# Two layers of pair updates on one core: an affine step cut from four rows to two, and moments of a running output aggregated per sixteen rows

## The reference

```
x = x + L0(_gn(x))      # L0: g * (_ln(einsum('bikc,bkjc->bijc', a, b)) @ Wz + bz),  g = sigmoid(xn @ Wg + bg)
x = x + L1(_gn(x))      # L1: layernorm, p = xn @ pi + b, gate = sigmoid(xn @ gi + b), h = p * gate * mask, triangles, ...
_gn(v) = (v - m) / sqrt(s + 1e-5)   # m, s: mean and variance of a group over all 512 x 512 positions
```

## Time and profile before

| | |
|---|---|
| median of three runs | 4713.67 us (4711.84 to 4716.98) |
| the profiled execution: its own time, its span | 4714.6 us, 4712.9 us |
| mean granted clock of TensorE | 0.975 |
| PE busy | 3987.0 us, 85% |
| DVE busy | 3935.2 us, 83% |
| ACT busy | 3377.8 us, 72% |
| POOL busy | 2670.3 us, 57% |
| HBM traffic over the span | 325 GB/s |

### The profile page before, as it was taken

One profiled execution on the slowest core, in us unless ns is written; L12 is line 12 of the kernel. 1 busy time (PEld: TensorE's weight loads), 2 busy tenths in 40 slices (PEclk: granted clock), 3 DMA queues, 4 the chain that ended last, 5 costly groups with the idle time before them and its releaser, 6 DMA issues. The chain is left out here.

```text
span 4712.9 us, 89415 instructions
## 1 busy us (share of the span) xinstructions
PE 3987.0 (85%) x26438; PEld 2239.9 (48%) x26438; DVE 3935.2 (83%) x5450; ACT 3377.8 (72%) x4840; POOL 2670.3 (57%) x1428
## 2 busy tenths in 40 slices
PE   0008999891999999799999999799999978888888
PEld 0005666441666666455555555355654434444444
DVE  5778888678888888899999999677789978777776
ACT  2337999553777777588888888566667768888887
POOL 0000000591888888588888888733334428888887
PEclk9999999995999999899999999899999989999999
DMA  9997999546999999799999999766678859999999
GB/s 366 410 405 261 364 369 366 176 134 202 392 391 390 390 390 391 268 311 319 321 322 321 320 320 322 271 230 223 231 254 305 305 186 406 407 403 405 403 402 354
DMA packets 700627, 1532.73 MB, mean 325 GB/s; under 512 B 32976, under 2 KB 50832, under 8 KB 698128
## 3 DMA queue, kind: packets, MB, share of 16 engines
q1 hardware_dynamic: 563696, 1263.31, 74.3%
q10 hardware_dynamic: 136864, 268.59, 14.9%
HBM read 1009.59 MB, written 522.19 MB: 325 GB/s over the span
## 5 line engine op out<-in xcount | busy, mean ns | idle before, releaser
L1766 POOL TENSOR_TENSOR s_oT<-s_gated,s7in_x1t 128x1024 f32<-128x1024 f32 x256 | 689.0, 2694 | 220.6 <-DVE s_gated L1685 215.4
L981 POOL TENSOR_TENSOR s_x1T<-s_gz,s_xT 128x512 f32<-128x512 f32 x512 | 652.1, 1274 | 127.9 <-DVE s_gz L947 123.2
L1432 PE MATMUL s_y_ps<-s_ab 128*128 128x512 f16 x3072 | 680.1, 380 | 2.0 <-DVE s_ab L1503 2.0
L1138 POOL TENSOR_TENSOR s_low<-s_xc,s_high 128x1024 f16<-128x1024 f32 x256 | 546.9, 2137 | 222.0 <-ACT s_high L1099 222.0
L878 PE MATMUL s_g_ps<-s_xT,s_Wg 128*128 128x512 f32 x1024 | 523.3, 593 | 0.0
L1685 DVE SCALAR_TENSOR_TENSOR s_gated<-s_p_ps,k_po_bias,s_gate 128x1024 f32<-128x1024 f32 x256 | 328.6, 1284 | 183.7 <-ACT s_gate L1722 164.0
L908 ACT ACTIVATE s_g<-s_g_ps,s_bg 128x512 f32<-128x512 f32 x512 | 351.7, 687 | 174.3 <-PE s_g_ps L878 174.3
L718 POOL MEMSET s_total<- 128x2048 f32 x1 | 1.8, 1809 | 837.9 <-POOLq L41 837.9
L1432 PEld LDWEIGHTS s_y_ps<-s_ab 128*128 128x128 f16 x3072 | 300.9, 98 | 344.8 <-issue 4.4
L947 DVE SCALAR_TENSOR_TENSOR s_gz<-s_z_ps,k_z_bias,s_g 128x512 f32<-128x512 f32 x512 | 384.4, 751 | 88.8 <-ACT s_g L908 86.5
L1104 ACT ACTIVATE s_gate<-s_g_ps,k_gi_bias 128x1024 f32<-128x1024 f32 x256 | 284.1, 1110 | 186.1 <-PE s_g_ps L1272 185.7
(11 more groups left out here) (225 smaller groups left out, 9499.8 us busy)
## 6 DMA issues: line engine op xcount, KB each, us to landing
s2in_xt<-in_x SPq DMA_DIRECT2D x128, 1024.0 KB, 9.6
s_xt<-in_x SPq DMA_DIRECT2D x256, 512.0 KB, 7.3
x_d<-s_x1T ACTq DMA_DIRECT2D x128, 1024.0 KB, 9.6
s5in_xt<-x_d SPq DMA_DIRECT2D x128, 1024.0 KB, 9.1
h_d<-s_h SPq DMA_DIRECT2D x128, 1024.0 KB, 6.8
s7in_x1t<-x_d SPq DMA_DIRECT2D x128, 1024.0 KB, 13.9
out<-s_ot ACTq DMA_DIRECT2D x128, 1024.0 KB, 9.3
s_mask_b<-mask_d SPq DMA_DIRECT2D x128, 512.0 KB, 4.8
```

Of the source, the lines that this page charges most:

```text
L981: pool.tensor_tensor(x1T[:, i // U, i % U, :], gz[:, i % 4, :], xT[:, i % 8, :], ALU.add).then_inc(added, 1)
L1138: pool.tensor_tensor(low[:, n % 4, :, :], xc[:, n % 4, :, :], high[:, n % 4, :, :], ALU.subtract).then_inc(rest_ready, 1)
L1432: last = pe.matmul(y_ps[:, ib, 0:N], ab[:, u % 2, 0, a, kb, ib * P:(ib + 1) * P], ab[:, u % 2, 1, b, kb, :], start=m == 0, stop=m == len(t ...
L1766: pool.tensor_tensor(oT[:, n % 4, :, :], gated[:, n % 4, :, :], x1t[:, n // 2, 2 * (n % 2):2 * (n % 2) + 2, :], ALU.add).then_inc(added, 1)
```

## The change

Stage 4: the tile of statistics holds 16 rows and is used again in every body. At the start of a body DVE waits for the last statistics of the body before, does the mix of row 2, aggregates the 16 rows into a mean and a variance (`gather`, one `bn_aggr` of 96 numbers into `last_mv`), and goes on with statistics of row 0, which wait until `gather` is done. After the statistics of row 1 it copies the two numbers to their place (`place`, a copy of two elements per partition). The body's first statistics find a tile that was set to 1.0 ahead of the loop. At the end of the stage the last 16 rows are gathered, and the 32 means and variances are combined by six short instructions instead of one long and three short ones.

Stage 5: the affine step handles two rows instead of four. It is issued in every step but n = 4 and 12 (with the square root); step 7 and step 15 carry two of them. The total of rows is the same. The affine of a pair waits for the load of its whole group, as before.

```
--- before.py
+++ after.py
@@ -804,8 +804,9 @@
         g = s.sbuf("g", [P, 2, N])
         gz = s.sbuf("gz", [P, 4, N])
         x1T = s.sbuf("x1T", [P, GROUPS, U, N])
-        stats = s.sbuf("stats", [P, N, 6])
-        mv = s.sbuf("mv", [P, 2])
+        stats = s.sbuf("stats", [P, ROWS, 6])
+        last_mv, mv = s.sbuf("last_mv", [P, 2]), s.sbuf("mv", [P, N // ROWS, 2])
+        wide = s.sbuf("wide", [P, 2, N // ROWS])
         pair = s.sbuf("pair", [P, 2])
         Wg = s.sbuf("Wg", [P, P])
         bg = s.sbuf("bg", [P, 1])
@@ -813,8 +814,8 @@
         g_ps = s.psum("g_ps", [P, 2, BANK])
         z_ps = s.psum("z_ps", [P, 2, BANK])
         loaded, z_loaded, stored = s.sems("loaded", GROUPS), s.sems("z_loaded", GROUPS), s.sems("stored", GROUPS)
-        turned, kept, g_prod, z_prod, sig, mixed, added, counted = [
-            s.sem(n) for n in ("turned", "kept", "g_prod", "z_prod", "sig", "mixed", "added", "counted")]
+        turned, kept, g_prod, z_prod, sig, mixed, added, counted, gathered, placed = [
+            s.sem(n) for n in ("turned", "kept", "g_prod", "z_prod", "sig", "mixed", "added", "counted", "gathered", "placed")]
         padded, folded, shifted, moments_ready, chain = s.sem("padded"), s.sem("folded"), s.sem("shifted"), s.sem("moments_ready"), s.sem("chain")
 
         @block_of(nc)
@@ -887,7 +888,7 @@
                 for i in range(ROWS):
                     step(N // ROWS - 1, i, last=True)
 
-                pe.wait_ge(chain, 3)
+                pe.wait_ge(chain, 4)
                 for m in range(2):
                     pe.matmul(moments[:, m:m + 1], K.group_mean[:], pair[:, m:m + 1], start=True, stop=True).then_inc(moments_ready, 1)
 
@@ -935,10 +936,20 @@
 
                 def statistics(r, i):
                     dve.wait_ge(added, r * ROWS + (i + 9))
-                    dve.bn_stats(stats[:, bass.ds(r * ROWS + i, 1), :].rearrange("p a s -> p (a s)"),
-                                 x1T[:, i // U, i % U, :]).then_inc(counted, 1)
-
-                dve.sem_inc(counted, ROWS)
+                    if i == 0:
+                        dve.wait_ge(gathered, r + 1)
+                    if i == U:
+                        dve.wait_ge(placed, r + 1)
+                    dve.bn_stats(stats[:, i, :], x1T[:, i // U, i % U, :]).then_inc(counted, 1)
+
+                def gather():
+                    dve.bn_aggr(last_mv[:], stats[:].rearrange("p n s -> p (n s)")).then_inc(gathered, 1)
+
+                def place(r):
+                    dve.wait_ge(gathered, r + 1)
+                    dve.tensor_copy(mv[:, bass.ds(r, 1), :].rearrange("p a s -> p (a s)"), last_mv[:]).then_inc(placed, 1)
+
+                dve.memset(stats[:], 1.0).then_inc(counted, ROWS)
 
                 def mix(r, i):
                     dve.wait_ge(sig, r * ROWS + (i + 1))
@@ -948,9 +959,15 @@
                                              ALU.add, ALU.mult).then_inc(mixed, 1)
 
                 def step(r, i, last=False):
+                    if i == 0:
+                        dve.wait_ge(counted, r * ROWS + ROWS)
                     if not (last and i + 2 >= ROWS):
                         mix(r, i + 2)
+                    if i == 0:
+                        gather()
                     statistics(r, i)
+                    if i == 1:
+                        place(r)
 
                 mix(0, 0)
                 mix(0, 1)
@@ -960,12 +977,18 @@
                 for i in range(ROWS):
                     step(N // ROWS - 1, i, last=True)
                 dve.wait_ge(counted, N + ROWS)
-                dve.bn_aggr(mv[:], stats[:].rearrange("p n s -> p (n s)")).then_inc(chain, 1)
+                gather()
+                dve.wait_ge(gathered, N // ROWS + 1)
+                dve.tensor_copy(mv[:, 0, :], last_mv[:]).then_inc(placed, 1)
+                dve.wait_ge(placed, N // ROWS + 1)
+                dve.tensor_copy(wide[:, 0, :], mv[:, :, 0])
+                dve.tensor_tensor(wide[:, 1, :], mv[:, :, 0], mv[:, :, 0], ALU.mult).then_inc(chain, 1)
                 dve.wait_ge(chain, 1)
-                dve.tensor_copy(pair[:, 0:1], mv[:, 0:1])
-                dve.tensor_tensor(pair[:, 1:2], mv[:, 0:1], mv[:, 0:1], ALU.mult).then_inc(chain, 1)
+                dve.tensor_tensor(wide[:, 1, :], wide[:, 1, :], mv[:, :, 1], ALU.add).then_inc(chain, 1)
                 dve.wait_ge(chain, 2)
-                dve.tensor_tensor(pair[:, 1:2], pair[:, 1:2], mv[:, 1:2], ALU.add).then_inc(chain, 1)
+                dve.tensor_reduce(pair[:], wide[:], AX.X, ALU.add).then_inc(chain, 1)
+                dve.wait_ge(chain, 3)
+                dve.tensor_scalar(pair[:], pair[:], ROWS / N, None, ALU.mult).then_inc(chain, 1)
                 norm_vector(dve)
 
             @block.gpsimd
@@ -1075,11 +1098,12 @@
                 act.sem_inc(parts_turned, 1)
                 act.sem_inc(sig, 1)
 
-                def affine(r, k):
-
-                    r, k = r + k // GROUPS, k % GROUPS
+                def affine(r, n):
+
+                    r, n = r + n // PAIRS, n % PAIRS
+                    k, two = n // 2, slice(n % 2 * 2, n % 2 * 2 + 2)
                     act.wait_ge(loaded[k], r * 16 + 16)
-                    act.activation(xt[:, k, :, :], xt[:, k, :, :], ACT.Identity, bias=K.gn_shift[:], scale=K.gn_scale[:]).then_inc(affined, 1)
+                    act.activation(xt[:, k, two, :], xt[:, k, two, :], ACT.Identity, bias=K.gn_shift[:], scale=K.gn_scale[:]).then_inc(affined, 1)
 
                 def deviation(r, b):
                     act.wait_ge(counted, r * BODY + (16 * b + 18))
@@ -1111,17 +1135,19 @@
                         deviation(r, (n + 4) // BLOCK)
                     if n % BLOCK == 5 and not (last and n + 3 >= PAIRS):
                         keep_rows(r, (n + 3) // BLOCK)
-                    if n % 2 == 1 and not (last and n + 1 + LEAD >= PAIRS):
-                        affine(r, (n + 1 + LEAD) // 2)
-
-                for k in range(4):
-                    affine(0, k)
+                    for m in ((2,), (2,), (2,), (2,), (), (1,), (1,), (1, 2))[n % BLOCK]:
+                        if not (last and n + m + LEAD >= PAIRS):
+                            affine(r, n + m + LEAD)
+
+                for n in range(BLOCK):
+                    affine(0, n)
                 act.wait_ge(eps_ready, 1)
                 deviation(0, 0)
-                affine(0, 4)
+                for n in range(BLOCK, BLOCK + 2):
+                    affine(0, n)
                 keep_rows(0, 0)
-                for k in range(5, LEAD // 2 + 1):
-                    affine(0, k)
+                for n in range(BLOCK + 2, LEAD + 2):
+                    affine(0, n)
                 round_high(0, 0)
                 round_high(0, 1)
                 act.activation(unused[:], K.bg[:], ACT.Sigmoid)
@@ -1239,8 +1265,7 @@
 
                 def turn(r, n):
 
-                    if n % 2 == 0:
-                        pe.wait_ge(affined, r * GROUPS + (n // 2 + 1))
+                    pe.wait_ge(affined, r * PAIRS + (n + 1))
                     for row in range(2 * n, 2 * n + 2):
                         pe.wait_ge(counted, r * BODY + (row + 1))
                         for q in range(CB):
```

## The result

The changed kernel takes 4789.94 us (median of 4 runs, 4786.09 to 4791.19), the kernel before 4712.81 us in the same session (4711.84 to 4716.98). The ratio is 1.0161, 95% interval 1.0143 to 1.0178: 77 us slower. The forecast was 4795, range 4755 to 4812. The profiled execution of after takes 4791.19 us, its span is 4789.3, the mean granted clock 0.976.

What follows compares the result with a forecast made beforehand. PE and DVE were taken to have almost no slack in stage 5, with a narrow 0.17 us in stage 4's loop. Terms -7.2 + 24.6 - 2.5 + 66 = +81 us gave 4795 against the median, range 4755 to 4812.

Steps and rivals of the forecast that it cites:

- End of stage 4: Stage 4 to 5 border: chain 12.9 us shorter, but the barrier waits for the last store, so only -7.2 us.
- Inside stage 4: Stage-4 loop: aggregation and a copy held by POOL cost PE 0.77 us per body, 32 times: +24.6 us.
- the reading of L1188: Stage-4 loop: the two-element copy is held until POOL's operation ends, like a 64-element DVE instruction taking 0.44 instead of 0.20 us.
- Start of stage 5: Before stage 5's loop: half affines take some 1.05 us instead of 2.08, so PE starts earlier: -2.5 us.
- Loop of stage 5: Stage-5 loop: affines moved a step earlier meet unlanded loads, 2.2 us per half body, 30 times: +66 us.
- first stall: Stage-5 loop, step 8: ACT waits for an unlanded load, the gate is 2.35 us late, PE loses 2.0 to 2.2.
- (a): Rival, stage 4: the two-element copy is not held up by POOL; +62 us, 4776; chance 0.25.
- (b): Rival, stage 5: the affine's earlier wait does not stall, only stage 4 counts; +15 us, 4729; chance 0.04.
- (c): Rival: shorter stage-4 end pays, the rest is hidden; -4 us, 4710; chance 0.04.
- (d): Rival, stage 5: delayed ACT also delays the square root, second stall counts fully; 84 us instead of 66, 4813; chance 0.09.
- second stall: Stage-5 loop, step 10: ACT meets the next group's unlanded load, gate some 0.5 us late, 0.1 counted.
- The second form of (c): Stage 4 to 5 border: besides, the barrier does not wait for the store; end gives 12.9 instead of 7.2 us, 4704.

Runs made afterwards that it cites:

- s4_reduce_place: Stage-4 half of the change alone, against the kernel before, with the two numbers placed by a sum over a one-element axis instead of a copy: 4717.29 us, ratio 1.0005.
- s5_only: Stage-5 half of the change alone, stage 4 as in the kernel before: 4771.73 us, ratio 1.0122 to the kernel before.
- s5_early_loads: Stage-5 half of the change alone, against the kernel before, with SP issuing each group's load two steps earlier: 4710.57 us, ratio 0.9994.
- s5_old_place: Stage 4 and loads as in the kernel before; affine in halves, both at the step where the whole group stood: 4719.34 us, ratio 1.0010.

## Why the prediction was right

The likeliest case of the forecast came true, 5 us above the time measured. By stretches, each of the four terms is found where it was put, and the two large ones have the cause that they were given. Inside the two loops the terms are added up from parts of which some were too high and others too low; there the close sum is partly luck.

- **End of stage 4**, -7.2: measured -7.3. The floor by the last store, and not the 12.9 of the chain, is what decides: DVE is done 5.4 us before the store has landed.
- **Inside stage 4**, +24.6: measured +25.3. Carrying the reading of L1188 over to a copy of two elements held: 0.86 us in the loop, 0.17 at the end, 0.14 for another operation at the same place. The Trainium skill (SBUF — State Buffer, Who interferes with whom) says that a copy in a two-port mode, issued second, is fully blocked until GpSimd's instruction is over, and names no size below which it is not; no row names the mode of this copy, but its times agree. The split is less exact than the sum. The hold was put at 18.6 us and is worth 16.4; the rest was put at 6 and is 8.7 in s4_reduce_place. Per body of that kernel (means of 28) the wait for the last statistics, put at nothing, costs 0.03, mix(3) comes 0.38 later behind mix(2) instead of 0.36, and 0.14 is regained instead of 0.17. The aggregation takes 0.58 us instead of the 0.53 of the earlier trace rows, and statistics(0) begins 1.28 behind mix(2) instead of 1.24. PE's weight load waits twice a body, after mix(3) too, where once was forecast.
- **Start of stage 5**, -2.5: measured -2.6.
- **Loop of stage 5**, +66: measured +63.6, and 58.6 in s5_only. Per half body 2.1 and 2.0 us where I took 2.2. s5_early_loads shows that the late loads are behind all of it. But the 2.2 was split wrongly: 2.1 for the first stall, which PE was to keep almost whole, and 0.1 for the second. From one `s_h` to the next, after against s5_early_loads (means of 28 half bodies), the step of the first stall is 1.55 us longer and that of the second 0.91, and after each some 0.2 is regained: 1.4 and 0.7. The first wait is shorter than taken, 2.2 us in the mean and not 3.1 (2229.4 - 2226.33), as the loads land 8.5 us after issue in the median and ACT comes 6.7 behind the issue instead of 6.0 in the row shown; the second is as long as the first. The two errors cancel, and that the term fits so well is luck.
- **Rivals.** (a), the copy not held, falls with s4_reduce_place. (b) and (c) needed loads that land within 5.85 us; ACT waited 59 times. (d) had 84 where 63.6 were measured; but its mechanism, a second stall that counts, is there with 0.7 us per half body, and only the shorter first stall keeps the sum down. The second form of (c), an opening that does not wait for the store, falls too: B is 11.4 or 11.5 us in every kernel with the short tail.
- **Wrong in size.** The half affine takes 1.23 us, not 1.05: I halved a duration that has a fixed part (two halves are 2.36 in one row, the whole is 2.08). Behind a half that has waited for its load this moves the gate by the full 0.18; ACT's wait does not hide it. Where a double step stands ahead of the square root it makes the 12 us of s5_old_place and s5_spread_later. ACT's waits for loads were forecast at over 150 us, 50 times; they were 126.3 us, 59 times, in 30 first and 29 second stalls of 2.2 and 2.1 us in the mean.
- The sum is 79.0 by the stretches against 81 forecast, of which D has -2.4 and A +0.7.

## What to carry to other kernels

Work moved out of a serial tail into a loop costs what the loop's slack does not hide (4.5 us for 19.1 us of aggregation here, 25 us with a copy that is held), and what it saves in the tail ends at the next thing that the barrier awaits (7.3 us here, where the chain became 12.7 shorter): look both up before cutting. An instruction that reads a load sets the load's deadline; moved ahead by one step, it needs its load ahead by a step too, and in the queue of its engine what stands behind it pays (61 us here, all of it back when SP issues the loads two steps earlier). A two-number move beside a busy GpSimd belongs on GpSimd itself, or in an operation that is not held: both were tried here, and both take the hold away. A forecast that fits in its sum is not yet right in its parts: the steps of the loop, laid beside a run without the cost, show which stall was paid.

## What the runs showed of the hardware

- How long a short VectorE instruction takes depends on the phase in which it meets POOL. The `s_parts` conversion (64 elements) has a mean of 403 ns before, 801 in after, 807 in s5_only and 203 in s5_old_place, always the same instruction. In after the one issued at 2242.14 us takes 0.92 and ends 0.05 us behind an operation of POOL that runs from 2240.88 to 2243.01; in s5_old_place the one at 2245.70, 0.09 us before the end of POOL's operation, takes 0.20. From the groups of instructions of after and of s5_old_place:

```profile
L1214 DVE TENSOR_SCALAR s_parts<-s_rstd 128x64 f16<-128x64 f32 x32 | 25.6, 801 | 1.1
```

```profile
L1191 DVE TENSOR_SCALAR s_parts<-s_rstd 128x64 f16<-128x64 f32 x32 | 6.5, 203 | 1.1
```

- A `tensor_reduce` of the same two fp32 numbers is not held: 134 to 140 ns over its 32 executions.
